# A transformer block with causal attention and experts: fours of heads on row groups in turn, no filler matmuls, the mask written first

## The reference

```
scores = k @ q / sqrt(8), causal, 16 heads of 8;  probs = softmax(scores);  out = (probs @ v) @ Wo
ffn:     h = gelu(bq(xn) @ bq(Wfc) + b);  y = bq(h) @ bq(Wproj) + b
         bq: blocks of 32 share an exponent, mantissas rounded to 3 bits
experts: sum over 8 of (silu(xn @ Wg) * (xn @ Wu)) @ Wd,  128 -> 512 -> 128
```

## Time and profile before

| | |
|---|---|
| profiled execution | 1633.84 us, its span 1632.1 us |
| busy | PE 1501.3 us (92%), DVE 1036.6 (64%), ACT 823.3 (50%), POOL 678.2 (42%) |
| layer 0, 120 to 640 us, 13 windows of 40 us | PE busy 36.9 to 39.9 us of 40, mean granted clock 0.88 (0.74 to 1.00) |
| layer 1, 1000 to 1100 us | PE busy 98.35 us of 100, DVE 78.46, clock 1.00 |
| fillers (L147), whole kernel | 384 matmuls, 132.4 us busy |

### The profile page before, as it was taken

One profiled execution on the slowest core, in us unless ns is written; L12 is line 12 of the kernel. 1 busy time (PEld: TensorE's weight loads), 2 busy tenths in 40 slices (PEclk: granted clock), 3 DMA queues, 4 the chain that ended last, 5 costly groups with the idle time before them and its releaser, 6 DMA issues. The chain is left out here.

```text
span 1632.1 us, 23537 instructions
## 1 busy us (share of the span) xinstructions
PE 1501.3 (92%) x8440; PEld 840.4 (51%) x8440; DVE 1036.6 (64%) x2379; ACT 823.3 (50%) x1220; POOL 678.2 (42%) x791
## 2 busy tenths in 40 slices
PE   2899999999999999369999999999999999999987
PEld 1444444444444443245656656666666566666655
DVE  3545655565655453157876767777777677777743
ACT  2335455555545445135655556555655565555650
POOL 4222324243333223245554455454545554545440
PEclk9559888898979789679999999999999999999997
DMA  3312223232413221231010110111111101111003
GB/s 118 85 35 74 73 82 93 68 98 71 125 56 106 79 64 61 72 92 54 28 52 27 31 47 28 34 48 36 32 53 32 43 28 35 32 37 32 18 14 111
DMA packets 59025, 93.95 MB, mean 58 GB/s; under 512 B 12119, under 2 KB 22876, under 8 KB 56862
## 3 DMA queue, kind: packets, MB, share of 16 engines
q1 hardware_dynamic: 57902, 92.00, 18.9%
q10 hardware_dynamic: 1008, 0.46, 0.1%
HBM read 50.08 MB, written 40.11 MB: 55 GB/s over the span
## 5 line engine op out<-in xcount | busy, mean ns | idle before, releaser
L1133 POOL TENSOR_TENSOR a_h_lo<-a_h,a_h_hi 128x512 fp32r<-128x512 f32 x256 | 329.2, 1286 | 143.6 <-ACT a_h_hi L1180 134.2
L668 DVE TENSOR_REDUCE l_mx<-bank_pair 128x2 f32<-128x1024 f32 (+1 forms) x192 | 200.0, 1044 | 237.7 <-PE bank_pair L886 236.5
L1241 DVE SCALAR_TENSOR_TENSOR a_h<-a_h,bank_pair 128x512 f32<-128x512 f32 x256 | 175.6, 686 | 171.9 <-ACT a_h L1176 169.0
L749 ACT ACTIVATE l_E<-bank_pair 128x1024 f32<-128x1024 f32 (+1 forms) x192 | 169.3, 883 | 179.3 <-PE bank_pair L139 178.8
L192 POOL TENSOR_SCALAR_AFFINE_SELECT l_E<-l_E 128x256 f32<-128x256 f32 (+1 forms) x192 | 95.6, 500 | 382.0 <-ACT l_E L749 382.0
L1187 ACT ACTIVATE a_E<-bank_pair 128x1024 f32<-128x1024 f32 (+1 forms) x192 | 169.8, 884 | 166.5 <-PE bank_pair L139 166.3
L168 DVE CUSTOM_DVE_ANT_0 bank_pair<-bank_pair,mask 128x512 f32<-128x512 f32 (+3 forms) x512 | 238.0, 516 | 7.1 <-PE bank_pair L129 6.9
L1180 ACT ACTIVATE a_h_hi<-a_h 128x512 fp32r<-128x512 f32 x256 | 160.6, 627 | 115.5 <-DVE a_h L1247 115.5
L192 POOL TENSOR_SCALAR_AFFINE_SELECT a_E<-a_E 128x256 f32<-128x256 f32 (+1 forms) x192 | 95.0, 495 | 281.6 <-ACT a_E L1187 281.5
L1247 DVE TENSOR_TENSOR a_h<-a_h,bank 128x512 f32<-128x512 f32 x256 | 176.0, 688 | 27.0 <-DVE a_h L1241 0.5
L1176 ACT ACTIVATE a_h<-bank_pair 128x512 f32<-128x512 f32 x256 | 151.6, 592 | 72.8 <-PE bank_pair L1319 69.2
(11 more groups left out here) (134 smaller groups left out, 2379.1 us busy)
## 6 DMA issues: line engine op xcount, KB each, us to landing
st<-stack_d SPq DMA_DIRECT2D x112, 128.0 KB, 3.1
st<-stack_d SPq DMA_DIRECT2D x224, 64.0 KB, 3.0
stack_d<-l_q_k_hi SPq DMA_DIRECT2D x48, 256.0 KB
stack_d<-l_q_k_lo SPq DMA_DIRECT2D x32, 256.0 KB
o_d<-l_O SPq DMA_DIRECT2D x32, 256.0 KB, 2.0
o_d<-a_O SPq DMA_DIRECT2D x32, 256.0 KB, 2.0
l_st<-stack_d SPq DMA_DIRECT2D x16, 128.0 KB, 3.6
l_st<-stack_d SPq DMA_DIRECT2D x32, 64.0 KB, 3.5
```

The costliest lines, as they stand in the source:

```text
L668: nc.vector.tensor_reduce(out, src, AX.X, ALU.max).then_inc(S_used, 1)
L749: nc.scalar.activation(E[:, pair % SLOTS_E, at_col:at_col + HALVES * w].rearrange("p (r c) -> p r c", r=HALVES), pair_of("T", g, n)[:, :, ...
L1133: nc.gpsimd.tensor_tensor(h_lo[:, q % RH, :], h[:, q % RH, :], h_hi[:, q % RH, :].bitcast(F32), ALU.subtract).then_inc(h_lo_ready, 1)
L1241: nc.vector.scalar_tensor_tensor(hq, hq, 1.0, g_bank[:, :], ALU.add, ALU.mult).then_inc(silu_ready, 1)
```

## The change

- A stack has 3 slots (24 rows) and 4 rows of maxima: 28 rows. The product low x low is no longer computed. A buffer holds two quads: even ones at partitions 0 and 64, odd ones at 32 and 96 (`row_of`, `buffer_of`). Both layers have 4 stacks in 2 buffers; a stack is loaded by 2 DMAs instead of 6, the parts of a projection are stored by 6 instead of 5.
- One function, `scores_and_keys`, issues S(g+1, n) and T(g, n) together, their matmuls interleaved, so that neighbours lie on different row groups. In layer 0 it makes both waits first, then writes the mask over the whole width of the S unit (identity times mask), and accumulates the scores on it. T(g, 0..5) is now in step g, PV(g) at its end, behind M(g+1).
- The fillers are gone.
- M is a matmul of the 8 columns of maxima with an fp32r identity, in place of a transposition of 72 columns.
- In layer 0 the tiles of the FFN run four steps later, `fc` a batch later; the weights' part of the FFN and the bias move from the first two steps to the fourth; the loads of wq, wk and their biases come first with a semaphore of their own. In step g, SP stores the outputs of g-1 (before g-2).

```diff
@@ -44,14 +44,12 @@
 HEADS_A_QUAD = PLANES * HALVES
 QUADS_A_BATCH = HEADS // HEADS_A_QUAD
 QUADS = QUADS_A_BATCH * B
-SLOTS = 4
+SLOTS = 3
 SLOT_ROWS, MROWS = SLOTS * HD, 4
 ROWS = SLOT_ROWS + MROWS
-PLAIN_ROWS, IMAGE_ROWS = 2 * HD, 3 * HD
-HALF = P // 2
+HALF, GROUP = P // 2, P // 4
 MAXIMA = HEADS_A_QUAD * 2
-M_COLS = HALF + MAXIMA
-IMAGE_SLOTS = (((0,), (0, 2)), ((1,), (1,)))
+IMAGE_SLOTS = (((0, 2), (0, 1)), ((1,), (2,)))
 RH, LAG = 4, 3
 NEG = -1.0e30
 LN_EPS = 1e-5
@@ -67,9 +65,9 @@
 EXP_AT = (0, 1024, 2048)
 COLS = 2560
 SLOTS_E = 3
-STACKS, MOE_STACKS = 4, 3
-FIRST, WQ, SMALL_LOADS, PART_STORES = -7, 2, 18, 16 * 5
-STACK_LOADS, MAX_LOADS = 16 * 3 * HALVES, 16 * HALVES
+STACKS, STACKS_A_BUFFER = 4, 2
+FIRST, WQ, FIRST_LOADS, SMALL_LOADS, PART_STORES = -7, 2, 4, 14, 16 * 6
+STACK_LOADS, MAX_LOADS = 16 * HALVES, 16 * HALVES
 
 
...
@@ -91,20 +89,29 @@
         self.eng.nop(nofuse=True)
 
 
-def load_stacks(sp, st, st_d, g, done):
-
-    image = st_d[g // QUADS_A_BATCH, g % QUADS_A_BATCH]
+def row_of(g, r):
+
+    return HALF * r + GROUP * (g % STACKS_A_BUFFER)
+
+
+def buffer_of(stacks, g):
+
+    return stacks[g // STACKS_A_BUFFER % len(stacks)]
+
+
+def load_stacks(sp, stacks, st_d, g, done):
+
+    image, st = st_d[g // QUADS_A_BATCH, g % QUADS_A_BATCH], buffer_of(stacks, g)
     for r in range(HALVES):
-        rows, at = image[IMAGE_ROWS * r:IMAGE_ROWS * (r + 1)], HALF * r
-        sp.dma_start(st[at:at + PLAIN_ROWS, :, :, :].bitcast(F32), rows[0:PLAIN_ROWS]).then_inc(done, 16)
-        sp.dma_start(st[at + PLAIN_ROWS:at + SLOT_ROWS, :, 0, :].bitcast(F32), rows[0:PLAIN_ROWS, :, 0, :]).then_inc(done, 16)
-        sp.dma_start(st[at + PLAIN_ROWS:at + SLOT_ROWS, :, 1, :].bitcast(F32), rows[HD:HD + PLAIN_ROWS, :, 1, :]).then_inc(done, 16)
-
-
-def load_maxima(sp, st, ms, g, done):
-
+        row = row_of(g, r)
+        sp.dma_start(st[row:row + SLOT_ROWS, :, :, :].bitcast(F32), image[SLOT_ROWS * r:SLOT_ROWS * (r + 1)]).then_inc(done, 16)
+
+
+def load_maxima(sp, stacks, ms, g, done):
+
+    st = buffer_of(stacks, g)
     for r in range(HALVES):
-        row = HALF * r + SLOT_ROWS
+        row = row_of(g, r) + SLOT_ROWS
         rows = ms[MROWS * r:MROWS * (r + 1), g % 2, :].unsqueeze(1).to_broadcast([MROWS, PLANES, N])
         sp.dma_start(st[row:row + MROWS, :, 0, :].bitcast(F32), rows).then_inc(done, 16)
...
@@ -121,24 +128,18 @@
     return nc.tensor.matmul(bank[:, :], sel[rows, b % 2, :], rden[rows, :], start=True, stop=True)
 
 
-def scores(nc, bank, st, n, r, j):
-
-    rows = slice(HALF * r, HALF * r + SLOT_ROWS)
-    for kb, col in UNITS[n]:
-        t, w = NT - 1 - kb, width(kb)
-        ins = nc.tensor.matmul(bank[:, col:col + w], st[rows, j, 0, bass.ts(t, P)], st[rows, j, 1, 0:w], start=True, stop=True)
-    return ins
-
-
-def keys_by_queries(nc, pair, st, n, j):
-
-    for kb, col in UNITS[n]:
-        w = width(kb)
-        for r in range(HALVES):
-            rows = slice(HALF * r, HALF * r + ROWS)
-            ins = nc.tensor.matmul(pair[:, r, col:col + w], st[rows, j, 1, bass.ts(kb, P)], st[rows, j, 0, N - w:N],
-                                   start=True, stop=True)
-    return ins
+def scores(nc, bank, stacks, g, r, block, first, last):
+
+    j, t, col = block
+    w, st, rows = P * (t + 1), buffer_of(stacks, g), slice(row_of(g, r), row_of(g, r) + SLOT_ROWS)
+    return nc.tensor.matmul(bank[:, col:col + w], st[rows, j, 0, bass.ts(t, P)], st[rows, j, 1, 0:w], start=first, stop=last)
+
+
+def keys_by_queries(nc, bank, stacks, g, r, j, block):
+
+    kb, col = block
+    w, st, rows = width(kb), buffer_of(stacks, g), slice(row_of(g, r), row_of(g, r) + ROWS)
+    return nc.tensor.matmul(bank[:, col:col + w], st[rows, j, 1, bass.ts(kb, P)], st[rows, j, 0, N - w:N], start=True, stop=True)
 
...
-
-        def transposed(back, n):
-            put(("T", g - back, n), 0 <= g - back < QUADS)
-
-        scores_of(0)
-        transposed(1, 3)
+            put(("T", g, n), 0 <= g < QUADS)
+
+        scores_and_keys(0)
         put(("V", 0, b + 1), u == 0 and 0 <= b + 1 < B)
         put(("K", 1, b - 2), u == 2 and 0 <= b - 2 < B)
         put(("Q", 0, b + 2), u == 3 and 0 <= b + 2 < B)
-        scores_of(1)
-        transposed(1, 4)
+        scores_and_keys(1)
         put(("X", 1, b - 2), u == 1 and 0 <= b - 2 < B)
         put(("V", 1, b - 2), u == 2 and 0 <= b - 2 < B)
         put(("K", 0, b + 2), u == 3 and 0 <= b + 2 < B)
-        scores_of(2)
-        transposed(1, 5)
+        scores_and_keys(2)
+        scores_and_keys(3)
+        scores_and_keys(4)
+        scores_and_keys(5)
+        put(("F", b, 0), u == 0 and 0 <= b < B)
+        put(("F", b, 1), u == 0 and 0 <= b < B)
+        put(("Q", 1, b - 2), u == 1 and 0 <= b - 2 < B)
         put(("X", 0, b + 2), u == 2 and 0 <= b + 2 < B)
-        scores_of(3)
-        transposed(0, 0)
-        scores_of(4)
-        transposed(0, 1)
         put(("A", 1, b - 1), u == 3 and 0 <= b - 1 < B)
-        put(("Q", 1, b - 2), u == 1 and 0 <= b - 2 < B)
-        scores_of(5)
-        transposed(0, 2)
-        put(("F", b + 1, 0), u == 0 and 0 <= b + 1 < B)
-        put(("F", b + 1, 1), u == 0 and 0 <= b + 1 < B)
         put(("M", g + 1, 0), 0 <= g + 1 < QUADS)
...
@@ -362,7 +354,7 @@
 
         def tile_of(g):
 
-            return g + 3 if 0 <= g + 3 < NT * B else None
+            return g - 1 if 0 <= g - 1 < NT * B else None
 
...
+            first = [(wq[0][:, :], wq0_in), (wk[0][:, :], wk0_in), (bq[:, :], bq_in), (bk[:, :], bk_in)]
+            for to, source in first:
+                sp.dma_start(to, source).then_inc(w0_in, 16)
             small = [(wfc_n, wfc_in.rearrange("(c p) k -> p c k", p=P)), (wpj_n, wpj_in), (bfc32, bfc_in),
...
@@ -867,39 +867,47 @@
                 if place[unit] >= 3:
                     pe.wait_ge(*read_out(*order[place[unit] - 3]))
 
-            def S(g, n):
-                if n == 0:
-                    pe.wait_ge(stack_in[g % STACKS], STACK_LOADS * (g // STACKS + 1))
-                    if g == 0:
-                        pe.wait_ge(set_up, 2)
-                begin("S", g, n)
-                pair = pair_of("S", g, n)
+            def scores_and_keys(g, n):
+
+                more, here = in_range(g + 1), in_range(g)
+                if more:
+                    if n == 0:
+                        pe.wait_ge(stack_in[(g + 1) % STACKS], STACK_LOADS * ((g + 1) // STACKS + 1))
+                        if g + 1 == 0:
+                            pe.wait_ge(set_up, 2)
+                    begin("S", g + 1, n)
+                if here:
+                    if n == 0:
+                        pe.wait_ge(mrow_in, MAX_LOADS * (g + 1))
+                    begin("T", g, n)
                 t = NT - 1 - n % 2 if n < 4 else 5 - n
-                w = P * (t + 1)
-                for j in ((n // 2,) if n < 4 else range(PLANES)):
-                    at_col = j * N // PLANES if n >= 4 else 0
+                score_blocks = [(n // 2, t, 0)] if n < 4 else [(j, t, j * N // PLANES) for j in range(PLANES)]
+                key_blocks = UNITS[n % 3]
+                if more:
+                    blocks, w = len(score_blocks), P * (t + 1)
                     for r in range(HALVES):
-                        rows = slice(HALF * r, HALF * r + SLOT_ROWS)
-                        nc.tensor.matmul(pair[:, r, at_col:at_col + w], st[g % STACKS][rows, j, 0, bass.ts(t, P)],
-                                         st[g % STACKS][rows, j, 1, 0:w], start=True, stop=False)
+                        bank = pair_of("S", g + 1, n)[:, r, :].rearrange("p (j c) -> p j c", j=blocks)[:, :, 0:w]
+                        part = mask[:, N - w:N].unsqueeze(1).to_broadcast([P, blocks, w])
+                        nc.tensor.matmul(bank, identb[:, :], part, start=True, stop=False)
+                for k in range(2):
                     for r in range(HALVES):
-                        ins = nc.tensor.matmul(pair[:, r, at_col + w - P:at_col + w], identb[:, :], mask[:, N - P:N], start=False, stop=True)
-                ins.then_inc(S_ready, 1)
+                        if more and k < len(score_blocks):
+                            ins = scores(nc, pair_of("S", g + 1, n)[:, r, :], stacks, g + 1, r, score_blocks[k], False, k == len(score_blocks) - 1)
+                            if r == HALVES - 1 and k == len(score_blocks) - 1:
+                                ins.then_inc(S_ready, 1)
+                    for r in range(HALVES):
+                        if here and k < len(key_blocks):
+                            ins = keys_by_queries(nc, pair_of("T", g, n)[:, r, :], stacks, g, r, n // 3, key_blocks[k])
+                            if r == HALVES - 1 and k == len(key_blocks) - 1:
+                                ins.then_inc(T_ready, 1)
 
             def maxima_rows(g):
                 begin("M", g, 0)
                 bank = bank_of("M", g, 0)
                 pe.wait_ge(nm_ready, g + 1)
                 for t in range(NT):
```

(88 more changed lines are left out.)

196 lines of the change are left out of this document (88 added, 108 removed).

## The result

The changed kernel takes 1694.57 us (median of 4 runs, 1691.99 to 1699.97), the kernel before 1633.41 beside it: ratio 1.038, 95% interval 1.0325 to 1.044. Its profiled span is 1692.4 us against 1632.1, 60.3 more. The times of the first and the last M of each layer say where.

What follows compares the result with a forecast made beforehand. Layer 0 was to turn from near-gapless TensorE to alternating scores and VectorE reductions: 1633.8 + 121 (layer 0) - 30 (layer 1) - 10 (start) - 2 (layer 1's start) = 1713 us, range 1615 to 1790.

Steps and rivals of the forecast that it cites:

- Joint waits in layer 0: Layer 0 slots: masks, scores and keys by queries wait for VectorE's previous reduction, so they alternate; wide slot 2.34 us.
- The hand-off: Layer 0 step end: the maxima's way from M to T(g,0) takes 4.3 us, some 1.4 of it uncovered.
- The clock: Layer 0: falls in each step, rises in each PV; half the work at either level, 19.3 and 25.8 us, so 22.5.
- Removing the fillers buys nothing here: Layer 0: dropping 3.1 us of fillers a step gains nothing, since TensorE has some 7 us to wait in anyway.
- Layer 1: Scores and keys by queries of a slot overlap on four row groups; 0.9 us a quad saved, -30 us.
- if the waits give way: Layer 1's best bound, -57 us: VectorE's waits would not limit the 1.8 us a quad the joined groups save.
- Start: Kernel start: first store of parts at 20.7 us instead of 29.61, and two issues saved; -10 us, bounds 0 and -13.
- Edges: Layer 1's start: stacks load in two issues instead of six, -2 us.
- the clock that stays up: Rival, layer 0: full-width masks do what the fillers did and PV is near; 1614 us, chance 0.17.
- the one that stays down: Rival, layer 0: the clock is down nearly always, step 25.8 us, kernel 1815 us; chance 0.15.
- the groups that don't run together: Rival, layer 1: the four row groups do not overlap and layer 1 gives nothing; 1743 us, chance 0.09.
- TensorE as the bound: Rival, layer 0: reductions somehow overlap and TensorE's work of 12.0 us a step bounds it; 1387 us, chance 0.04.

Runs made afterwards that it cites:

- d: The changed kernel with layer 0's two waits of a slot taken apart, scores first, then keys by queries: 1571.2 us, 0.964 of the kernel before.
- b: Run a (old order, new stacks) with the twelve fillers of a step left out: 1617.5 us, 0.990 of the kernel before.
- e: The changed kernel with the twelve fillers put back behind layer 0's joint waits, ahead of the masks: 1785.3 us, 1.092 of the kernel before.
- i: Run a with all quads on the row groups beginning at rows 0 and 64, so scores and keys by queries cannot overlap: 1601.9 us, 0.983.
- q: Run i with layer 1's keys by queries over 36 stack rows instead of 28, the further rows zeros: 1633.9 us, 1.002.
- k: Run a with the change's early start (small weights first, weights turned a step later), tiles and FC left in place: 1581.4 us, 0.971.
- a: The kernel before's layer 0 order, waits, masks and fillers, with the change's stacks, row groups, M and whole layer 1: 1587.4 us, 0.973.
- h: Run a with layer 0's wait of keys by queries put ahead of its slot's masks and scores, a joint wait: 1658.2 us, 1.019.
- g: Run d with the fillers of before behind the second wait, ahead of keys by queries: 1600.7 us, 0.984 of the kernel before.

## Why the prediction was right, step by step

**Joint waits in layer 0.** The sum put scores and reductions in turn, 2.34 us for a wide slot at the upper level. The trace has them in turn, a slot pair at 405.42 and 408.30 with a clock between the levels, and d shows the wait is the cause. Mechanism shown; the step 22.15 us for the 22.5 forecast, +109 for +121. VectorE's wait ahead of a reduction was 1.85 us in the mean (355.3 us for 192), where about 1 was named.

**The hand-off** was oversized: 1.4 us a step naked. T's masks waited for it 20.5 us in 15 of the 32 steps, where most were forecast, 0.64 a step, and with split waits 8.9 in all.

**The clock.** Forecast half of the work at either level, about 0.75; 0.69 came. What it costs was priced at 3.2 us a step on top of 19.3. The means of the kernels do not show it: d's clock is 0.75 and its step is shorter than that of before at 0.86; b lost 0.8 us a step with 0.17 of clock and twelve fillers gone. Steps of one kernel with the same work (four steps apart, as many instructions) do show that 0.2 of clock less costs 3 to 4 us. In d the step from 339.95 us takes 16.9 at 0.90, and the one from 413.45 us 20.5 at 0.67, with 1.5 and 1.3 us idle. In e the step from 522.70 us takes 20.9 at 0.91 and the one from 419.08 us 24.2 at 0.71, with 4.3 and 3.8 idle. So the size of the price is plausible. What is not shown is how much of it the changed kernel pays: none of its 31 steps ran above 0.83, and no run raised its clock and left its chain alone, since e added its fillers to the chain. How the 3.5 us over the old step divide between waiting and slow chain links stays open, and the forecast's "half of the work at either level" was a choice, not a derivation: that the step came so near it is in part luck.

**"Removing the fillers buys nothing here"** holds only if they would stand in the pause. Behind the joint wait, where e has them, leaving them out is worth 3.1 us a step.

**Layer 1**: -41.5 for -30, and the failed step is the sentence that 28 rows cost and save nothing, "TensorE streams the same columns". i to q prices the 36 rows at 33 us in the interleaved order. In the order of before they are worth some 24.5, if nothing else counts: the 28.0 us from before to i, less 3.5 for M, which as matmuls of 8 columns takes 0.24 us where the four transposes took 0.35 (1205.71 to 1206.06 before), 0.11 x 32.

The overlap, to which all 30 were given, is worth some 12 to 16 us, 0.4 to 0.5 a quad for the 0.9 forecast. A wide slot did fall from 0.86 us to 0.43, as the sum had it, but less of that by the overlap: i without it takes 0.68. Nor did VectorE's slack hold the gain to 0.9 us a quad. Between the first and the last M of layer 1 TensorE's busy time fell by 46 us (825.4 to 779.1) and its idle time rose by 5 only (17.7 to 22.5); the gate matmuls wait for VectorE 7.9 us in all, 38 times in 256, where they waited 7.0 us before. Of the 57 us that the prediction gave as the bound "if the waits give way", most came.

A joined group takes 0.43 to 0.44 us, as long as a pair of 512 columns by itself before. The Trainium skill ("TensorE: Matmul & The Clock Gate", Part 3) gives 3.07 as the speedup of four row tiles; the 0.06 us more that the prediction worked out from it does not show in these rows.

**Start**: -13.1 for -10, with the cause half right. The store left at 18.88 us as argued (20.7 was forecast), but k shows that this alone gives nothing; what stood ahead of the scores in TensorE's own queue was left out of the sum.

**Edges**: -2 forecast for layer 1's start, +5.8 came from layer 0's last M to layer 1's first M. Layer 1's first scores still waited 15.0 us for a stack. In a, with the old order, this stretch is 83.9 us (626.1 to 710.0), so the increase comes with what a and after share, the stacks, M and the new layer 1, and not with the order. The rest was not tried.

Of the rivals, the clock that stays up is excluded by 0.69, the one that stays down by 22.15 us a step, the groups that don't run together by 0.43 us; TensorE as the bound is excluded for the changed kernel by its 5.9 idle us a step and by a time 308 us over the 1387 it gave.

## What to carry to other kernels

When two units of a software pipeline are issued as one group, the group waits for the later of their waits: look up what each wait is released by, and how long the unit ahead of it has been in the queue. Issue the unit with the early release first and put the other's wait behind its matmuls: here the same change without the joint wait is 3.6% faster than the kernel before, the best version run, and with it 3.8% slower. A pause costs twice where it brings the clock down: in h a step with 1.1 us more of waiting ran 8.9 us longer. Price fillers by where they stand: in the old order they won 30 us (a, b), ahead of keys by queries with split waits they lost 30 (g), and behind a wait that a chain goes through they cost their whole length (e), even if the clock rises.

## What the hardware showed that was not expected

- In h two pauses of 0.45 and 0.66 us were followed by matmuls at the lower level, and the step took 25.0 us for 16.2 of the same work.
- Matmuls of 24 and of 36 rows next to each other cost 1.05 us for a slot that takes 0.68 with 24 and 28 rows and 0.43 with those on four row groups.
- A granted clock of 0.95 with fillers (g) was slower than 0.75 without (d), 1600.7 us for 1571.2.
- Fillers that made TensorE's busy time of a step 18% longer (19.3 for 16.3 us) raised the clock from 0.69 to 0.74 only (e).
